# Mixing stage: the phases are made by GpSimd, and the products stand ahead of the powers

## The chip, the cores and the metric

The kernel runs on one core of one Trainium2 chip. The core has five engines with queues of their own: PE (TensorE, matrix products into the memory PSUM), DVE (VectorE), ACT (ScalarE), POOL (GpSimd) and SP, which here only issues transfers. They wait for one another by semaphores. The metric is the device time of one execution in microseconds (us), the median of three runs.

## The reference

A tower of one layer works on `x` of 32 x 128 x 64 complex numbers. A diagonal state space kernel makes 1024 positions out of 64 complex coefficients per row; then come attention with rotary positions and a layer with weights and activations rounded to 8 bits, each with a residual.

```python
dtA = A * dt[:, None]                      # A = -exp(inv_A_real) + 1j * A_imag, dt = exp(log_dt)
Cc = Bc[None, :, :] * Cc                   # Cc = x as complex numbers: (32, 128, 64)
Cc = Cc * (jnp.exp(dtA) - 1.0) / A
V = jnp.exp(dtA[:, :, None] * ell)         # ell = 0 .. 1023: (128, 64, 1024)
h = 2.0 * jnp.einsum('chn,hnl->chl', Cc, V).real
h = concatenate([cls_tok, h], axis=1)      # (32, 129, 1024)
h = h + attention(layernorm(h))            # 32 heads of 32, 8 for keys and values, causal
h = h + ffn(layernorm(h))                  # 1024 x 1024, both factors rounded to 8 bits, and a bias
```

## The kernel before

`program` runs three stages one behind the other: `mix_stage`, `attention_stage`, `ffn_stage`. The change touches `mix_stage` alone, which computes the einsum above.

A position l is split into a block j of 8 and an offset of 128 (PB) within it. For a row h the power exp(dtA * l) is the product of a block factor, which goes into the coefficients (tables `gr`, `gi`, turned by PE into `g_ps`), and a power of the offset, which goes into `eb`. The 128 rows h are worked in 8 chunks (NCP) of 16 (CP), each chunk k in two halves of 8 (CH). For one chunk:

- phases: for each of the 16 rows, one instruction iota * rate + quarter, 128x128, into `yb` (in pool_b). `turns_of`, DVE, L427.
- rounding: `kb`, the nearest whole number of the phases, 128x2048 (in pool_a). DVE, L432.
- subtraction: `yb` - `kb`, the fraction of a turn. POOL, L284. It waits for `wholes` and, by a second wait, for powers of the chunk before.
- sine: `sn` = sin(2 pi * fraction), 128x2048. ACT, L376, with a change of its function table before and after. For rows of even number the quarter turn makes it a cosine.
- magnitudes: 16 exponentials of 128x128 into `eb`. ACT, L368.
- powers: `eb` = `eb` * `sn`, 128x2048, both from SBUF. DVE, L422.
- products ("coefficients" in the code): `m1`, `m2` = input times coefficient, for one half of the chunk, two instructions of 128x2048, one factor from `g_ps` in PSUM. DVE, L523. They wait until PE has used up the same half of the chunk before (`rows_ready`).
- matrix products: per half four units of 8 matmuls of 128x128 into four PSUM banks. PE, L342; the profile records each as two. A unit waits until ACT has emptied its bank (`rows_out`).
- copies: ACT empties each bank into `ho` (L400), and SP stores it to `h_rows` in HBM, four stores a half.

`eb` has three buffers, `yb` two, `kb` and `sn` one, `m1` and `m2` one for each half. The order on each engine is written out by hand, and each engine works through its queue strictly in that order. DVE's order in a chunk is: phases and rounding of chunk k + 2, powers of chunk k + 1, both halves of products of chunk k + 1. ACT puts the magnitudes of chunk k + 2 behind the copies of the first half of chunk k, four rows a copy, and the sine of k + 2 behind them.

Before the loop there is a set-up of many small DVE instructions (exponentials, the coefficient tables through the helper `times`, copies into `dup`) beside the transposes of the input; its end is the turning of `dup` into `g_ps`, 16 transposes (L324), which wait for the whole of `dup` (`turn_in`).

Of the kernel before, what the change touches and what calls it, by code (L numbers as in the profile page):

```python
# [27 lines left out]
ALU = mybir.AluOpType  # L28
# [8 lines left out]
JB = 8  # L37
# [75 lines left out]
def at_least(eng, sem, value):  # L113

    if isinstance(value, int) and value <= 0:
        return
    eng.wait_ge(sem, value)
# [46 lines left out]
def mix_stage(nc, x, log_dt, B, inv_A, A_im, consts, h_dram, pool_a, pool_b, cst, ident_b, half_c, rows_stored,  # L164
# [6 lines left out]
    with ExitStack() as ctx:  # L171
# [3 lines left out]
        def sem(name):  # L175
            return ctx.enter_context(nc.semaphore("mix_" + name))
# [55 lines left out]
        turn_in = sem("turn_in")  # L232
        turned = sem("turned")
        turned_out = sem("turned_out")
        turns = sem("turns")
        wholes = sem("wholes")
        fracs = sem("fracs")
        mags = sem("mags")
# [37 lines left out]
        @block.gpsimd  # L276
        def _(pool):
            nc.gpsimd.memset(warm[:], 0.0).then_inc(warm_set, 1)
            nc.gpsimd.memset(warm_r[:].bitcast(F32), 0.0).then_inc(warm_set, 1)
            nc.gpsimd.memset(half_c[:], -0.5)  # L280
            for k in range(1, NCP):
                pool.wait_ge(wholes, k + 1)
                at_least(pool, powers_ready, k)
                nc.gpsimd.tensor_tensor(yb[:, k % 2], yb[:, k % 2], kb[:], ALU.subtract).then_inc(fracs, 1)  # L284

        @block.tensor
        def _(pe):
            pe.wait_ge(warm_set, 2)
            for j in range(4):
                nc.tensor.matmul(ps[0][32 * j:32 * j + 32, 0:2 * PB], warm[:, 0:32], warm[:], start=True, stop=True)  # L290
            for i in range(2):
                for j in range(4):
                    nc.tensor.matmul(ps[j][:, i * PB:(i + 1) * PB], warm_r[32 * j:32 * j + 32, 0:P],
                                     warm_r[32 * j:32 * j + 32, 0:PB], start=True, stop=True)

            pe.wait_ge(cst_loaded, 16)
            for r, (kind, i) in enumerate(TURNS):
                if kind == "x":
                    pe.wait_ge(x_loaded[i], 16)
                if kind == "small":  # L300
                    pe.wait_ge(turn_in, 1)
                if kind == "swap":
                    pe.wait_ge(turned_out, XR + 1)
                if r >= OUT_BANKS:
                    pe.wait_ge(turned_out, r - OUT_BANKS + 1)
                bank = ps[r % OUT_BANKS]
                if kind == "swap":
                    hs = NH // XR
                    mm = nc.tensor.matmul(bank[:], swap, c1[:, i * hs:(i + 1) * hs, :].rearrange("p h c -> p (h c)"),
                                          start=True, stop=True)  # L310
                elif kind == "x":
                    for q in range(4):
                        mm = nc.tensor.transpose(bank[:, q * P:(q + 1) * P],
                                                 xin[:, 4 * i + q].rearrange("h n r -> h (n r)"), ident)
                else:
                    for q, slot in enumerate((S_DECAY, S_TURN)):
                        mm = nc.tensor.transpose(bank[:, q * P:(q + 1) * P],
                                                 dup[:, slot].rearrange("h n r -> h (n r)"), ident)
                mm.then_inc(turned, 1)
            pe.wait_ge(turn_in, 2)  # L320
            for i in range(G_TURNS):
                for q in range(4):
                    part, slot = divmod(4 * i + q, JB)
                    mm = nc.tensor.transpose(g_ps[:, part, slot, :],  # L324
                                             dup[:, 4 * i + q].rearrange("h n r -> h (n r)"), ident)
                mm.then_inc(turned, 1)
            pe.wait_ge(turned_out, len(TURNS))

            for k in range(NCP):
                pe.wait_ge(powers_ready, k + 1)  # L330
                for half in range(2):
                    pe.wait_ge(products, 2 * k + half + 1)
                    for i in range(PAIRS):
                        at_least(pe, rows_out, unit(k, half, i) - OUT_BANKS + 1)
                        bank = ps[i]
                        for e in range(2):
                            for jj in range(2):
                                h = 2 * i + e
                                slots = slice(jj * (JB // 2), (jj + 1) * (JB // 2))
                                cols = slice((2 * e + jj) * PB, (2 * e + jj + 1) * PB)  # L340
                                for term in (m1, m2):
                                    mm = nc.tensor.matmul(bank[:, cols],  # L342
                                                          term[:, half, h, slots].rearrange("p j c -> p (j c)"),
                                                          eb[:, k % 3, half * CH + h, :],
                                                          start=term is m1, stop=term is m2)
                        mm.then_inc(rows_ready, 1)

        @block.scalar
        def _(act):
# [23 lines left out]
            def sine(k):  # L373
                act.wait_ge(fracs, k + 1)
                at_least(act, powers_ready, k)
                nc.scalar.activation(sn[:], yb[:, k % 2], ACT.Sin, scale=TWO_PI_DOWN).then_inc(sin_done, 1)  # L376
# [13 lines left out]
                magnitudes(0, 2 * i, 2)  # L390
            sine(0)
            magnitudes(1, 0, CP)
            sine(1)
            for k in range(NCP):
                for half in range(2):
                    if k >= 1:
                        act.wait_ge(rows_stored[half], 16 * JB // 2 * k)
                    for i in range(PAIRS):
                        act.wait_ge(rows_ready, unit(k, half, i + 1))
                        nc.scalar.copy(ho[:, half, 2 * i:2 * i + 2, :],  # L400
                                       ps[i][:].rearrange("p (e q) -> p e q", e=2)).then_inc(rows_out, 1)
                        if half == 0 and k + 2 < NCP:
                            magnitudes(k + 2, 4 * i, 4)
                    if half == 0 and k + 2 < NCP:
                        sine(k + 2)

        @block.vector
        def _(v):
            count = [0]

            def link(ins):

                count[0] += 1
                ins.then_inc(small, 1)
                v.wait_ge(small, count[0])
# [5 lines left out]
                v.wait_ge(sin_done, k + 1)  # L421
                V.tensor_tensor(eb[:, k % 3], eb[:, k % 3], sn[:], ALU.mult).then_inc(powers_ready, 1)  # L422

            def turns_of(k):
                at_least(v, sin_done, k - 1)
                for h in range(CP):
                    t = V.tensor_scalar(yb[:, k % 2, h, :], iota, rates[:, 1, k * CP + h:k * CP + h + 1],  # L427
                                        quarter, ALU.mult, ALU.add)
                t.then_inc(turns, 1)
                v.wait_ge(turns, k + 1)  # L430
                at_least(v, fracs, k)
                V.tensor_scalar(kb[:], yb[:, k % 2], MAGIC, -MAGIC, ALU.add, ALU.add).then_inc(wholes, 1)  # L432
                if k == 0:
                    v.wait_ge(wholes, 1)
                    V.tensor_tensor(yb[:, 0], yb[:, 0], kb[:], ALU.subtract).then_inc(fracs, 1)

            v.wait_ge(in_loaded, 48)

# [52 lines left out]
            V.scalar_tensor_tensor(s1[:], s1[:], 2.0, den[:], ALU.mult, ALU.mult)  # L491
            link(V.scalar_tensor_tensor(s2[:], s2[:], -2.0, den[:], ALU.mult, ALU.mult))

            def times(re, im, t, ar, ai, br, bi):

                V.tensor_tensor(re, ar, br, ALU.mult)
                link(V.tensor_tensor(t, ai, bi, ALU.mult))
                link(V.tensor_tensor(re, re, t, ALU.subtract))
                V.tensor_tensor(im, ar, bi, ALU.mult)
                link(V.tensor_tensor(t, ai, br, ALU.mult))  # L500
                link(V.tensor_tensor(im, im, t, ALU.add))
# [4 lines left out]
            for q in range(2):  # L506
                last = V.tensor_tensor(wj[:, q], wj[:, q], mag[:], ALU.mult)
            link(last)
            many = [P, JB - 1, NS]
            times(gr[:, 1:JB], gi[:, 1:JB], tw[:], gr[:, 0:1, :].to_broadcast(many), gi[:, 0:1, :].to_broadcast(many),  # L510
                  wj[:, 0], wj[:, 1])

            V.tensor_copy(dup[:, 0:JB, :, 0], gr[:])
            V.tensor_scalar(dup[:, 0:JB, :, 1], gr[:], -1.0, None, ALU.mult)
            for q in range(2):
                last = V.tensor_scalar(dup[:, JB:2 * JB, :, q], gi[:], -1.0, None, ALU.mult)
            last.then_inc(turn_in, 1)
# [12 lines left out]
            v.wait_ge(turned, ROUNDS)  # L530
            v.wait_ge(turned_out, len(TURNS))
            coefficients(0, 0)
            turns_of(1)
            coefficients(0, 1)
            for k in range(NCP):
                if k + 2 < NCP:
                    turns_of(k + 2)
                if k + 1 < NCP:
                    powers(k + 1)
                    coefficients(k + 1, 0)  # L540
                    coefficients(k + 1, 1)


def attention_stage(nc, cls, h_dram, ctx_dram, tail_dram, ml_dram, v0_dram, pool_a, x_end_r, weights_r, cst, half_c, h_stored,
# [1189 lines left out]
```

## Time and profile before

| | |
|---|---|
| median of 3 runs | 1680.6 us (1679.89 to 1681.06) |
| profiled execution | 1692.2 us |
| its span, first to last instruction | 1690.4 us |
| busy over the span: PE, DVE, ACT, POOL | 93%, 72%, 53%, 36% |
| chunk loop of the mixing stage, first to last matmul | 44.7 to 190.5 us |
| first matmul of the attention stage | 194.4 us |
| stores of the mixed rows | 64 of 256 KB, median 3.7 us from issue to landing |

The profiled execution is a run of its own and longer than the median by 11.6 us. PE's share hides what happens in the mixing stage, since that is a ninth of the span; there, the times of single instructions have to be read. A busy time is the sum of the drawn lengths, and matmuls are pipelined, so the step between them is shorter than their length. PEclk is the granted clock of TensorE as a share of 2.4 GHz: 0.50 is 1.2 GHz.

### The profile page before, as it was taken

Reading aid. Unit: us, or ns where it says so; the run is one execution under the profiler, and the core shown is the slowest. Engines: PE = TensorE matmul, PEld = TensorE weight load, DVE = VectorE, ACT = ScalarE, POOL = GpSimd, SP = SyncE. Lnnn points to the kernel's source line nnn. Section 1 sums busy time; section 2 is a strip of 40 time slices with the busy share of each in tenths; the row PEclk is TensorE's granted clock in tenths of the full one; section 3 lists DMA queues with packets and bytes.
Section 4 is the critical chain, followed back from the end, with each engine's and each line's share of the span. In section 5 each row is a group of like instructions: output and inputs, shape, how many; then the busy total and the mean of one; then the engine's idle time right before and its main releaser. Section 6 shows DMA issues by size and latency. Waiting matters only on the chain. (4 is left out here: it accounts for less than half of the span.)

```text
span 1690.4 us, 35578 instructions
## 1 busy us (share of the span) xinstructions
PE 1576.1 (93%) x11802; PEld 1254.9 (74%) x11802; DVE 1213.1 (72%) x2262; ACT 888.1 (53%) x2928; POOL 615.0 (36%) x632
## 2 busy tenths in 40 slices
PE   4888889999999999999999999937799999999997
PEld 2788868888888888888888888826577777777774
DVE  8997556676767666676767666537588888888885
ACT  7576427777777777777777777722311111111110
POOL 0322024444444444444444444410133333333333
PEclk8889989999999999999999999958899999999998
DMA  8345501101010101101010100043233233332221
GB/s 211 75 104 121 150 26 39 44 33 50 25 50 31 43 31 43 47 28 50 25 50 31 43 31 20 27 184 125 90 112 101 96 101 112 112 111 100 94 92 44
DMA packets 59160, 122.64 MB, mean 73 GB/s; under 512 B 9345, under 2 KB 29954, under 8 KB 59106
## 3 DMA queue, kind: packets, MB, share of 16 engines
q1 hardware_dynamic: 59106, 121.94, 23.1%
q8 instruction: 32, 0.52, 0.1%
q14 instruction: 22, 0.18, 0.0%
HBM read 71.18 MB, written 51.66 MB: 73 GB/s over the span
## 5 line engine op out<-in xcount | busy, mean ns | idle before, releaser
L764 POOL TENSOR_TENSOR pool_a<-pool_a,ri 128x512 f32<-128x512 f32 x256 | 266.4, 1041 | 459.4 <-DVE ri L1126 459.4
L984 ACT ACTIVATE pool_a<-sm,ml 128x128 f32<-128x128 f32 x1024 | 399.4, 396 | 19.7 <-DVE ml L1119 18.7
L836 PE MATMUL att_ps<-w_lo,xT_hi 128*128 128x512 f32 x768 | 325.9, 424 | 0.0
L836 PE MATMUL att_ps<-w_hi,xT_lo 128*128 128x512 f32 x768 | 304.2, 396 | 0.0
L836 PE MATMUL att_ps<-w_hi,xT_hi 128*128 128x512 f32 x768 | 304.1, 396 | 0.0
L1110 DVE TENSOR_TENSOR sm<-att_ps,cst 128x512 f32<-128x512 f32 x256 | 173.3, 677 | 142.6 <-PE att_ps L884 142.6
L997 ACT COPY pool_a<-att_ps 128x512 f32<-128x512 f32 x256 | 149.5, 584 | 164.0 <-PE att_ps L893 164.0
L1435 PE MATMUL ffn_ps<-wo_hi,cT_hi 128*128 128x512 f32 x528 | 215.6, 408 | 3.0 <-DVE cT_lo L1578 3.0
L1435 PE MATMUL ffn_ps<-wo_hi,cT_lo 128*128 128x512 f32 x528 | 206.8, 392 | 0.0
L1435 PE MATMUL ffn_ps<-wo_lo,cT_hi 128*128 128x512 f32 x528 | 206.0, 390 | 0.0
L984 ACT ACTIVATION_READ_ACCUMULATOR pool_a<-sm,ml 128x1 f32 x1024 | 196.6, 192 | 0.0
L1119 DVE TENSOR_REDUCE ml<-sm 128x4 f32<-128x512 f32 x256 | 176.3, 689 | 9.1
L1535 ACT COPY pool_b<-ffn_psb 128x1024 bf16<-128x1024 bf16 x33 | 33.4, 1012 | 276.2 <-PE ffn_psb L1452 276.1
L836 PEld LDWEIGHTS att_ps<-w_lo,xT_hi 128*128 128x128 f32 x768 | 145.2, 189 | 35.5 <-issue 11.9
L836 PEld LDWEIGHTS att_ps<-w_hi,xT_hi 128*128 128x128 f32 x768 | 145.1, 189 | 33.9
L836 PEld LDWEIGHTS att_ps<-w_hi,xT_lo 128*128 128x128 f32 x768 | 145.8, 190 | 23.1
L893 PE MATMUL att_ps<-cst,pool_a 128*128 128x128 f32 x1024 | 157.9, 277 | 2.6 <-ACT pool_a L997 2.6
L893 PEld LDWEIGHTS att_ps<-cst,pool_a 128*128 128x128 f32 x1024 | 122.8, 141 | 36.9 <-issue 2.0
L342 PE MATMUL mix_ps<-eb,pool_b 128*128 128x128 f32 x1024 | 127.3, 291 | 23.1 <-ACT pool_b L400 18.5
L1418 POOL TENSOR_TENSOR pool_b<-pool_b 128x1024 f32<-128x1024 f32 x33 | 79.4, 2406 | 180.6 <-DVE pool_b L1604 164.7
L342 PEld LDWEIGHTS mix_ps<-eb,pool_b 128*128 128x128 f32 x1024 | 125.8, 207 | 24.8 <-issue 23.9
L1461 PE MATMUL ffn_ps<-wq,pool_b 128*128 128x512 bf16 x528 | 124.1, 390 | 2.2 <-ACT pool_b L1535 2.2
(213 smaller groups left out, 2510.5 us busy)
## 6 DMA issues: line engine op xcount, KB each, us to landing
h_in<-h_rows SPq DMA_DIRECT2D x33, 512.0 KB, 4.3
h_rows<-pool_b SPq DMA_DIRECT2D x64, 256.0 KB, 3.7
hbuf<-h_rows SPq DMA_DIRECT2D x32, 512.0 KB, 3.7
ctx_turned<-pool_a SPq DMA_DIRECT2D x64, 256.0 KB, 2.0
ctx_in<-ctx_turned SPq DMA_DIRECT2D x32, 512.0 KB, 3.6
out_dram<-pool_b SPq DMA_DIRECT2D x32, 512.0 KB, 2.8
pool_a<-in_L_attn_Wq_dram SPq DMA_DIRECT2D x8, 512.0 KB, 18.2
pool_b<-in_L_attn_Wo_dram SPq DMA_DIRECT2D x2, 2048.0 KB, 13.4
```

The lines of the kernel that those rows point to most:

```text
L342: mm = nc.tensor.matmul(bank[:, cols], term[:, half, h, slots].rearrange("p j c -> p (j c)"), eb[:, k % 3, half * CH + h, :], start=term i ...
L764: G.tensor_tensor(pr[:, g % 4], pr[:, g % 4], ri[:, g % 2, :].unsqueeze(2).to_broadcast([P, GQ, P]), ALU.mult).then_inc(p_ready, 1)
L836: mm = nc.tensor.matmul(bank[:], lhs, w_part[:, e, blk * BK:(blk + 1) * BK], start=(r == 0), stop=(r == EC * 3 - 1))
L893: mm = nc.tensor.transpose(PT_BANK[:, q * P:(q + 1) * P], pr[:, g % 4, q, :], ident)
L984: a = nc.scalar.activation(pr[:, g % 4, q, :], sm[:, g % 2, q, :], ACT.Exp, bias=ml[:, b[1], 0, h:h + 1], accum_out=ml[:, b[1], 1, h:h + 1])
L997: nc.scalar.copy(pT[:, g // 4, g % 4, :], PT_BANK[:]).then_inc(p_stored, 1)
L1110: V.tensor_tensor(sm[:, g % 2], S_BANK[g % 4][:].rearrange("p (q k) -> p q k", q=GQ), cst[:, C_MASK:C_MASK + P].unsqueeze(1).to_broadcast( ...
L1119: V.tensor_reduce(ml[:, b[1], 0, heads_of(g)], sm[:, g % 2], AX.X, ALU.max, negate=True).then_inc(negmax_ready, 1)
L1418: nc.gpsimd.tensor_tensor(yo[:, c[1], :], ya[:, c[1], :], hb[:, c[1], :], ALU.add).then_inc(out_ready, 1)
L1435: mm = nc.tensor.matmul(O_BANK[half][:], c_part[:, t[1], e, :], w_part[:, e, half * BK:(half + 1) * BK], start=(e == 0 and part == 0), sto ...
L1461: mm = nc.tensor.matmul(Y_BANK[half][:], xqT[:, c[1], e, :], wq8[:, e, half * BK:(half + 1) * BK], start=(e == 0), stop=(e == EC - 1))
L1535: nc.scalar.copy(xqT[:, c[1], :, :].rearrange("p c k -> p (c k)"), psb[:]).then_inc(xq_stored, 1)
```

## The change

Four edits, all in `mix_stage`. First, the phases of chunks 1 to 7 are made by POOL (L284 of the new file) instead of DVE; chunk 0's stay on DVE. POOL's queue becomes: wait for the first powers, phases of 1, and then for each chunk its subtraction and the phases of the next. The subtraction no longer waits for powers. Second, DVE's order in a chunk becomes: products of the first half, powers, rounding of the next chunk, products of the second half. Third, ACT spreads the magnitudes over both halves (four rows behind each of the first two copies of a half) and puts the sine of the next chunk behind the third copy of the first half; the second sine no longer comes before the loop. Fourth, in the set-up the real tables are written to `dup` as soon as the real part is there, and PE turns them while DVE makes the imaginary part.

```diff
@@ gpsimd
+            def phase(k):
+                at_least(pool, sin_done, k - 1)
+                for h in range(CP):
+                    t = nc.gpsimd.tensor_scalar(yb[:, k % 2, h, :], iota, rates[:, 1, k * CP + h:k * CP + h + 1],
+                                                quarter, ALU.mult, ALU.add)
+                t.then_inc(phases, 1)
+
+            def fraction(k):
+                pool.wait_ge(wholes, k + 1)
+                nc.gpsimd.tensor_tensor(yb[:, k % 2], yb[:, k % 2], kb[:], ALU.subtract).then_inc(fracs, 1)
+
+            pool.wait_ge(powers_ready, 1)
+            phase(1)
             for k in range(1, NCP):
-                pool.wait_ge(wholes, k + 1)
-                at_least(pool, powers_ready, k)
-                nc.gpsimd.tensor_tensor(yb[:, k % 2], yb[:, k % 2], kb[:], ALU.subtract).then_inc(fracs, 1)
+                fraction(k)
+                if k + 1 < NCP:
+                    phase(k + 1)
@@ tensor
-            pe.wait_ge(turn_in, 2)
             for i in range(G_TURNS):
+                if i % (G_TURNS // 2) == 0:
+                    pe.wait_ge(turn_in, 2 + 2 * i // G_TURNS)
@@ scalar
             magnitudes(1, 0, CP)
-            sine(1)
             for k in range(NCP):
                 for half in range(2):
...
-                        if half == 0 and k + 2 < NCP:
-                            magnitudes(k + 2, 4 * i, 4)
-                    if half == 0 and k + 2 < NCP:
-                        sine(k + 2)
+                        if i < 2 and k + 2 < NCP:
+                            magnitudes(k + 2, 8 * half + 4 * i, 4)
+                        if half == 0 and i == 2 and k + 1 < NCP:
+                            sine(k + 1)
@@ vector
-            def turns_of(k):
-                at_least(v, sin_done, k - 1)
-                for h in range(CP):
-                    t = V.tensor_scalar(yb[:, k % 2, h, :], iota, rates[:, 1, k * CP + h:k * CP + h + 1],
-                                        quarter, ALU.mult, ALU.add)
-                t.then_inc(turns, 1)
-                v.wait_ge(turns, k + 1)
+            def whole(k):
+                v.wait_ge(phases, k + 1)
                 at_least(v, fracs, k)
                 V.tensor_scalar(kb[:], yb[:, k % 2], MAGIC, -MAGIC, ALU.add, ALU.add).then_inc(wholes, 1)
...
+            def real_tables():
+                V.tensor_copy(dup[:, 0:JB, :, 0], gr[:])
+                V.tensor_scalar(dup[:, 0:JB, :, 1], gr[:], -1.0, None, ALU.mult).then_inc(turn_in, 1)
+
             times(gr[:, 1:JB], gi[:, 1:JB], tw[:], gr[:, 0:1, :].to_broadcast(many), gi[:, 0:1, :].to_broadcast(many),
-                  wj[:, 0], wj[:, 1])
-
-            V.tensor_copy(dup[:, 0:JB, :, 0], gr[:])
-            V.tensor_scalar(dup[:, 0:JB, :, 1], gr[:], -1.0, None, ALU.mult)
+                  wj[:, 0], wj[:, 1], real_tables)
+
...
             coefficients(0, 0)
-            turns_of(1)
+            whole(1)
             coefficients(0, 1)
-            for k in range(NCP):
-                if k + 2 < NCP:
-                    turns_of(k + 2)
+            for k in range(1, NCP):
+                coefficients(k, 0)
+                powers(k)
                 if k + 1 < NCP:
-                    powers(k + 1)
-                    coefficients(k + 1, 0)
-                    coefficients(k + 1, 1)
+                    whole(k + 1)
+                coefficients(k, 1)
```

How the rows of DVE move, from the first powers on. In the kernel before (L422 powers, L523 products, L427 phases, L432 rounding; `eb` the powers, pool_a the sine or the rounded phases, mix_g the coefficients in PSUM):

```order
L422 TENSOR_TENSOR eb<-eb,pool_a 128x2048
L523 TENSOR_TENSOR pool_b<-pool_b,mix_g 128x2048 x2
L427 TENSOR_SCALAR pool_b<-cst,rates 128x128 x16
L432 TENSOR_SCALAR pool_a<-pool_b 128x2048
L523 TENSOR_TENSOR pool_b<-pool_b,mix_g 128x2048 x2
L427 TENSOR_SCALAR pool_b<-cst,rates 128x128 x16
L432 TENSOR_SCALAR pool_a<-pool_b 128x2048
L422 TENSOR_TENSOR eb<-eb,pool_a 128x2048
L523 TENSOR_TENSOR pool_b<-pool_b,mix_g 128x2048 x4
```

And in the changed kernel (L435 powers, L541 products, L440 rounding):

```order
L435 TENSOR_TENSOR eb<-eb,pool_a 128x2048
L541 TENSOR_TENSOR pool_b<-pool_b,mix_g 128x2048 x2
L440 TENSOR_SCALAR pool_a<-pool_b 128x2048
L541 TENSOR_TENSOR pool_b<-pool_b,mix_g 128x2048 x4
L435 TENSOR_TENSOR eb<-eb,pool_a 128x2048
L440 TENSOR_SCALAR pool_a<-pool_b 128x2048
```

The phases are gone from DVE; of each four products two stand ahead of powers, and the rounding stands between powers and the other two.

On ACT, from the sine before the loop on. In the kernel before (L376 sine with its table, L368 magnitudes with theirs, L400 copies):

```order
L376 ACT_TABLE_LOAD
L376 ACTIVATE pool_a<-pool_b 128x2048
L400 COPY pool_b<-mix_ps 128x512
L368 ACT_TABLE_LOAD
L368 ACTIVATE eb<-cst,rates 128x128 x4
L400 COPY pool_b<-mix_ps 128x512
L368 ACTIVATE eb<-cst,rates 128x128 x4
L400 COPY pool_b<-mix_ps 128x512
L368 ACTIVATE eb<-cst,rates 128x128 x4
L400 COPY pool_b<-mix_ps 128x512
L368 ACTIVATE eb<-cst,rates 128x128 x4
L376 ACT_TABLE_LOAD
```

And in the changed kernel (L390 sine, L382 magnitudes, L413 copies), from the first copy on:

```order
L413 COPY pool_b<-mix_ps 128x512
L382 ACTIVATE eb<-cst,rates 128x128 x4
L413 COPY pool_b<-mix_ps 128x512
L382 ACTIVATE eb<-cst,rates 128x128 x4
L413 COPY pool_b<-mix_ps 128x512
L390 ACT_TABLE_LOAD
L390 ACTIVATE pool_a<-pool_b 128x2048
L413 COPY pool_b<-mix_ps 128x512 x2
L382 ACT_TABLE_LOAD
L382 ACTIVATE eb<-cst,rates 128x128 x4
L413 COPY pool_b<-mix_ps 128x512
L382 ACTIVATE eb<-cst,rates 128x128 x4
```

The sine stands behind the third copy now, and the other eight magnitudes behind the first copies of the second half.

## Rows read from the trace of the kernel before

**Rows 1.** Busy time by stage: the end of the set-up, the chunk loop.

```profile
36.20:44.70 8.50, 3.68 (x16) 3.28 (x17) 6.93 (x5) 3.63 (x9) 0.00 (x0) 0.50 0.05 12
44.70:190.50 145.80, 127.28 (x1024) 125.84 (x1024) 119.14 (x156) 89.91 (x179) 31.81 (x7) 0.91 0.46 109
```

**Rows 2.** Timeline of PE: start us, length us, line, what, xcount, [idle before].

```profile
36.38 3.68 PE L324 MATMUL mix_g<-cst,pool_b 128*128 128x128 f32 x16 [10.78 <-DVE pool_b L516]
44.73 9.10 PE L342 MATMUL mix_ps<-eb,pool_b 128*128 128x128 f32 x64 [4.67 <-DVE pool_b L523]
140.25 14.53 PE L342 MATMUL mix_ps<-eb,pool_b 128*128 128x128 f32 x128 [0.44 <-ACT pool_b L400]
159.14 31.32 PE L342 MATMUL mix_ps<-eb,pool_b 128*128 128x128 f32 x256 [4.36 <-ACT pool_b L400]
```

**Rows 3.** Waits, 36 to 192 us: who <- for whom, us, times, longest.

```profile
PE mix_ps L342 <- ACT pool_b L400: 18.5, 7, 5.0
ACT pool_a L376 <- POOL pool_b L284: 27.1, 7, 14.7
```

**Rows 4.** Timeline of DVE through one chunk, from 104 us.

```profile
104.58 4.49 DVE L523 TENSOR_TENSOR pool_b<-pool_b,mix_g 128x2048 f32<-128x2048 f32 x2 [2.66 <-PE mix_ps L342]
108.98 4.19 DVE L427 TENSOR_SCALAR pool_b<-cst,rates 128x128 f32<-128x128 f32 x16
113.20 1.23 DVE L432 TENSOR_SCALAR pool_a<-pool_b 128x2048 f32<-128x2048 f32 x1
114.34 2.28 DVE L422 TENSOR_TENSOR eb<-eb,pool_a 128x2048 f32<-128x2048 f32 x1
116.54 8.87 DVE L523 TENSOR_TENSOR pool_b<-pool_b,mix_g 128x2048 f32<-128x2048 f32 x4
```

**Rows 5.** Timeline of POOL and ACT in the same chunk.

```profile
116.77 4.53 POOL L284 TENSOR_TENSOR pool_b<-pool_b,pool_a 128x2048 f32<-128x2048 f32 x1 [15.40 <-DVE eb L422]
121.33 1.91 ACT L376 ACTIVATE pool_a<-pool_b 128x2048 f32<-128x2048 f32 x1 [3.35 <-POOL pool_b L284]
128.00 1.28 ACT L368 ACT_TABLE_LOAD   x1
```

**Rows 6.** Timeline of DVE, end of the set-up.

```profile
36.24 2.28 DVE L422 TENSOR_TENSOR eb<-eb,pool_a 128x2048 f32<-128x2048 f32 x1
40.09 4.49 DVE L523 TENSOR_TENSOR pool_b<-pool_b,mix_g 128x2048 f32<-128x2048 f32 x2 [1.57 <-PE mix_g L324]
```

**Rows 7.** Groups of small and large POOL instructions, and one of DVE.

```profile
L777 POOL COPY pool_a<-pool_a 128x4 f32 x52 | 9.9, 191 | 0.0
L278 POOL MEMSET warm<- 128x256 f32 x1 | 0.3, 311 | 0.3 <-POOLq L1723 0.3
L759 POOL TENSOR_TENSOR pool_a<-pool_a 128x256 f32<-128x256 f32 x32 | 23.7, 740 | 5.0 <-DVE pool_a L1092 5.0
L759 POOL TENSOR_TENSOR pool_a<-pool_a 128x512 f32<-128x512 f32 x64 | 81.7, 1276 | 6.3 <-DVE pool_a L1092 6.3
L435 DVE TENSOR_TENSOR pool_b<-pool_b,pool_a 128x2048 f32<-128x2048 f32 x1 | 2.3, 2293 | 0.0
```

**Rows 8.** Timeline of POOL: two instructions of one kind, one behind the other.

```profile
216.88 0.95 POOL L807 MEMSET x_end_hi<- 128x1024 f32 x1 [3.58 <-ACT w_hi L1037]
217.77 0.95 POOL L807 MEMSET x_end_lo<- 128x1024 f32 x1
```

**Rows 9.** DVE lines over the span: duration ns min/median/max, first and last start.

```profile
L1578 DVE TENSOR_TENSOR cT_lo<-ctx_in,cT_hi x64: 675/684/1879, 1159.4 to 1634.4; 128x512 fp32r<-128x512 f32 x64
L1585 DVE TENSOR_SCALAR pool_b<-pool_b,ffn_mv,ffn_rstd x33: 806/2873/2879, 1176.2 to 1669.7; 128x1024 f32<-128x1024 f32 x33
L523 DVE TENSOR_TENSOR pool_b<-pool_b,mix_g x32: 2280/2281/2289, 40.1 to 178.4; 128x2048 f32<-128x2048 f32 x32
```

**Rows 10.** Timeline of POOL and of DVE around 1265 us.

```profile
1265.53 2.39 POOL L1412 TENSOR_TENSOR pool_b<-pool_b,pool_a 128x1024 f32<-128x1024 f32 x1
1265.60 2.87 DVE L1585 TENSOR_SCALAR pool_b<-pool_b,ffn_mv,ffn_rstd 128x1024 f32<-128x1024 f32 x1 [0.67 <-POOL ffn_rstd L1408]
```

More of the change, by code:

```diff
@@ L234, in mix_stage @@
         turned_out = sem("turned_out")
-        turns = sem("turns")
+        phases = sem("phases")
         wholes = sem("wholes")
@@ L422, in powers, with turns_of @@
                 V.tensor_tensor(eb[:, k % 3], eb[:, k % 3], sn[:], ALU.mult).then_inc(powers_ready, 1)
-            def turns_of(k):
-                at_least(v, sin_done, k - 1)
-                for h in range(CP):
-                    t = V.tensor_scalar(yb[:, k % 2, h, :], iota, rates[:, 1, k * CP + h:k * CP + h + 1],
-                                        quarter, ALU.mult, ALU.add)
-                t.then_inc(turns, 1)
-                v.wait_ge(turns, k + 1)
+            def whole(k):
+                v.wait_ge(phases, k + 1)
                 at_least(v, fracs, k)
                 V.tensor_scalar(kb[:], yb[:, k % 2], MAGIC, -MAGIC, ALU.add, ALU.add).then_inc(wholes, 1)
-                if k == 0:
-                    v.wait_ge(wholes, 1)
-                    V.tensor_tensor(yb[:, 0], yb[:, 0], kb[:], ALU.subtract).then_inc(fracs, 1)
+            def turns_of(k):
+                for h in range(CP):
+                    t = V.tensor_scalar(yb[:, k, h, :], iota, rates[:, 1, k * CP + h:k * CP + h + 1],
+                                        quarter, ALU.mult, ALU.add)
+                t.then_inc(phases, 1)
+                whole(k)
+                v.wait_ge(wholes, k + 1)
+                V.tensor_tensor(yb[:, k], yb[:, k], kb[:], ALU.subtract).then_inc(fracs, 1)
             v.wait_ge(in_loaded, 48)
@@ L492, in _, with times @@
             link(V.scalar_tensor_tensor(s2[:], s2[:], -2.0, den[:], ALU.mult, ALU.mult))
-            def times(re, im, t, ar, ai, br, bi):
+            def times(re, im, t, ar, ai, br, bi, between=lambda: None):
                 V.tensor_tensor(re, ar, br, ALU.mult)
@@ L498, in times @@
                 link(V.tensor_tensor(re, re, t, ALU.subtract))
+                between()
                 V.tensor_tensor(im, ar, bi, ALU.mult)
```

## The prediction

> **What bounds the kernel now.** I read the busy time by stage first, then the timeline of PE, then who waited for whom, then DVE, POOL and ACT through one chunk. The change touches only the mixing stage. Its chunk loop runs from 44.7 to 190.5 us and holds 127.3 us of PE, 119.1 of DVE, 89.9 of ACT and 31.8 of POOL, at a granted clock of 0.91 [rows 1]: no engine is full. The timeline of PE says what full would be: an undisturbed chunk is 128 recorded matmuls in 14.5 us, while the first half chunk, after 4.7 us of idle, needs 9.1 us for 64, and the last two chunks, after a gap of 4.4 us, need 31.3 where undisturbed ones need 29 [rows 2]. So the loop's 145.8 us are about 8 x 14.4 = 115 us of work (14.5 less the drawn-out end of the last matmul), 18.5 us of gaps and some 12 us of matmuls at a lower clock. All seven gaps end with a copy of ACT, 18.5 us [rows 3]. ACT is late because it stands in front of its sine: 27.1 us it waited there for POOL's subtraction [rows 3]. One chunk shows the chain. DVE ends powers at 116.6, POOL's subtraction starts only then and takes 4.53 us, the sine starts at 121.3 [rows 4, 5]. DVE itself is what powers waits behind: per chunk 4.2 us of phases, 1.2 of rounding, 2.3 of powers and 8.9 of products [rows 4], 16.6 us before any wait, more than PE's 14.4. Two things hold the loop, then: DVE's load, and the chain powers, subtraction, sine, copies.
>
> **The change, part by part.**
>
> The set-up. The first eight transposes of the coefficients can start after the real tables, while DVE still makes the imaginary ones. Today all 16 run from 36.4 for 3.7 us at clock 0.50 [rows 1, 2] and DVE waits for them until 40.1, though its powers end at 38.5 [rows 6]. Eight will be over before 36.4, the other eight end near 38.2, so the first products start at 38.5 instead of 40.1: 1.6 us gained, and PE's first half chunk starts near 43.05 instead of 44.7. It comes after about as long an idle as now, so it keeps its 9.1 us.
>
> DVE. Seven times the 4.2 us of phases leave it (chunk 0's stay). 12.4 us per chunk remain, 2 us under PE's 14.4. The products of the first half now stand ahead of powers. The cycle that must close within a chunk is: PE does one half (7.2), which frees the product buffers; DVE makes the next products (4.5) and then powers (2.2 more); with 0.15 us of handing over (44.58 to 44.73, DVE's end to PE's start) this is 14.05. It closes with 0.35 us to spare. The rounding comes behind powers, and behind it the other half's products, which PE wants only half a chunk later: 1.2 + 4.4 us against 7.2.
>
> ACT. Its work per chunk is unchanged, 89.9 / 8 = 11.2 us [rows 1], but the exponentials are spread over both halves, and the sine comes behind the third copy of the first half. Each chunk still changes tables twice (1.28 us each [rows 5], in the 11.2). At that copy, 5.4 us into a chunk, the subtraction must be done: it is a rounding and 4.55 us behind powers, thus 5.8. The sine then ends about 9 us in, powers needs it at 12. The fourth copy is delayed to about 9.5, PE wants that bank back at 12.6. No wait of PE there.
>
> POOL. It takes over 7 x 16 phase instructions of 128x128, a form that no row shows here. I call its step from start to start t. From below: a copy of 4 elements takes 191 ns, and a memset grows from 311 ns for 256 elements to 0.95 us for 1024, 0.83 ns each; 191 + 124 x 0.83 = 0.29 us, of which 0.06 overlap with the next, since two memsets of 0.95 start 0.89 apart [rows 7, 8]. That is 0.23, with nothing for the two scalars read from memory. From above: two-tensor additions take 740 ns at 256 and 1276 at 512 elements, 2.09 each, so 0.47 at 128 [rows 7]. Another upper end: the 128x2048 subtraction takes 4.53 us on POOL and 2.29 on DVE [rows 5, 7], a ratio of 1.98, and DVE's phases step by 4.22 / 16 = 0.264 [rows 4]; that makes 0.52. Scalars from memory could put t above all of these. I take 0.38, midway between 0.29 and 0.47. 16t is then 6.1 us per chunk.
>
> What POOL's serial chain allows: in each chunk rounding (1.23), subtraction (4.55), phases of the chunk after next (16t), and powers (2.28), because the next rounding stands behind powers on DVE. The period is 8.06 + 16t, 14.15 us at t = 0.38: just under PE's 14.4. Written out from the end of the first powers: 38.5 + 7 x (1.23 + 4.55 + 16t) + 6 x 2.28 + 3.2 (last table and sine) + 2.3 (last powers) + 14.4 (last chunk on PE) = 112.6 + 112t. PE alone gives 43.05 + 9.1 + 7.2 + 7 x 14.4 = 160.2. The two meet at t = 0.425, and the chain reaches today's 190.5 at t = 0.70.
>
> Does POOL's reading hinder DVE? The rows say yes for two kinds of DVE instruction. One with a single tensor but a fast rate, 128x1024, takes 0.81 us undisturbed and 2.87 when POOL's 2.39 us addition started 0.07 us before it; one with two tensors from SBUF goes from 0.68 up to 1.88 [rows 9, 10]. The products read one tensor from PSUM, and all 32 keep 2.28 us although POOL's subtraction runs beside some [rows 9]. Powers reads two tensors from SBUF and now comes near POOL's phases. At t = 0.38 these end 5.8 + 6.1 = 11.9 us after the powers before, and powers wants to start at 12.0. If they meet, it waits for one phase instruction, 0.4 us at most, which the spare 0.35 nearly covers. I charge 0.15 us x 7 = 1 us.
> The Trainium skill, page "SBUF — State Buffer", section "Who interferes with whom", says this as a rule: a VectorE instruction with two SBUF inputs and a GpSimd one that reads SBUF shut each other out for a whole instruction. The trace agrees; by that rule the cost is the same 1 us, since each phase instruction is short.
>
> Transfers. The stores of the mixed rows kept the DMA engines at 0.46 of the loop [rows 1]; packed into 118 us that is 0.57, not a bound. The attention stage starts when the last rows are stored, at a fixed distance from the last copy, so what the loop gains arrives at the end of the program.
>
> Sum: the last matmul of the stage at 160.2 + 1 = 161.2 instead of 190.5, 29.3 us less. The profiled execution took 1692.2 us (span 1690.4), so 1662.9; it lies 11.6 us above the median of the runs, and I carry the difference over in microseconds: 1680.6 - 29.3 = 1651.
>
> **Rivals.**
>
> A, the forecast: PE becomes the bound, or POOL passes it by a hair, t up to 0.46. 1649 to 1655.
>
> B: POOL becomes the bound. For it: a kind of instruction it has not run here, and the ratio of 1.98 to DVE. At t = 0.523 the stage ends at 112.6 + 58.6 = 171.2, and the gain is 19.3: 1661. DVE then waits at the rounding with products behind it, and PE for the products. Against it: the ratio is that of two-tensor work, and POOL's small instructions are cheap. It holds from t = 0.46 to 0.67, 1655 to 1677.
> The Trainium skill, "GPSIMD Engine Reference", section "Engine selection", advises VectorE for elementwise work, calling GpSimd about twice as slow for two inputs but near line rate for one. By the factor of two for this kernel, B is what comes; by the one-input half of the sentence, A. Its section on elementwise cycle accounting has 769 ns for 512 elements in a good loop, from which I estimate 0.19 us for 128 and no delay at all. No run here shows either for this form.
>
> C, slower: the same instructions cost much more, because each fetches two scalars per partition. Place: POOL between subtraction and rounding. The price is 112 us for each microsecond of t, and it decides from t = 0.70. At t = 0.82 the stage ends at 204.4: 1694. If powers and phases did not exclude one another the chain would be 13.7 us shorter and the turning point 0.82. Against it: it needs nearly three times DVE's step.
>
> D: the gaps of PE stay in part, though POOL is quick enough. The sine still stands between two copies; if the subtraction comes a microsecond or two late there, or the clock drops again at each small gap, PE loses 1.5 us per chunk: 161.2 + 10.5 = 171.7, gain 18.8, 1662. For it: every gap today ends at a copy [rows 3], and the spare times above (0.35, 0.25 us) are thin. Against it: copies have 3 us of room through the four banks.
>
> **Chances.** A 0.57, B 0.26, C 0.08, D 0.09. The forecast is A's, 1651. What a measurement can tell here from no change is 0.2%, 3.4 us. C and half of B's far tail lie at or above that: faster 0.89, same 0.03, slower 0.08. For 8 in 10 the range takes in A with its lower bound (t = 0.23 gains nothing more, but powers undelayed and a first half at full clock would give 1646) and B and D up to t = 0.62: 1646 to 1671.
>
> **What would show it.** POOL's group of phase instructions: its mean and step give t at once. PE in the loop: 1024 matmuls without a gap above 1 us after the first chunk, granted clock near 1, the last ending near 161. ACT's wait for POOL before the sine falls from 27.1 us to a few. DVE's wait for POOL at the rounding: small in A, several us per chunk in B and C. Powers of 2.28 us stay so, or grow by up to 0.4 where phases run beside them. The set-up: first products at 38.5. I am wrong if t is above 0.46, or if PE waits more than 0.5 us per chunk for DVE or ACT while t is below that.

## The result, and the profile after

The changed kernel takes 1657.2 us (1656.5 to 1658.1, 4 runs) against 1680.4: a ratio of 0.9862, 95% interval 0.9845 to 0.9879, 23.2 us less. The forecast was 1651, 29.3 us less, in a range of 1646 to 1671.

PE in the mixing stage, the view of [rows 2] (timeline: start, length, what, xcount, idle before):

```profile
33.86 1.97 PE L338 MATMUL mix_g<-cst,pool_b 128*128 128x128 f32 x8 [8.32 <-DVE pool_b L528]
36.38 1.67 PE L338 MATMUL mix_g<-cst,pool_b 128*128 128x128 f32 x8 [0.56 <-DVE pool_b L534]
43.06 67.28 PE L356 MATMUL mix_ps<-eb,pool_b 128*128 128x128 f32 x576 [5.01 <-DVE pool_b L541]
110.67 14.56 PE L356 MATMUL mix_ps<-eb,pool_b 128*128 128x128 f32 x128 [0.32 <-DVE pool_b L541]
125.49 14.56 PE L356 MATMUL mix_ps<-eb,pool_b 128*128 128x128 f32 x128 [0.26 <-DVE pool_b L541]
140.31 21.71 PE L356 MATMUL mix_ps<-eb,pool_b 128*128 128x128 f32 x192 [0.26 <-DVE pool_b L541]
```

The stage's last matmul ends at 162.0 us (forecast 161.2, before 190.5). The seven gaps before ACT's copies are gone. PE runs its first 576 matmuls, four chunks and a half, without a gap; after that it waits 0.3 us for products once in each chunk.

POOL and DVE through one chunk, the views of [rows 4, 5]; the first row is POOL's very first set of phases:

```profile
38.63 6.88 POOL L284 TENSOR_SCALAR pool_b<-cst,rates 128x128 f32<-128x128 f32 x16 [37.30 <-DVE eb L435]
...
106.31 4.56 POOL L290 TENSOR_TENSOR pool_b<-pool_b,pool_a 128x2048 f32<-128x2048 f32 x1 [1.35 <-DVE pool_a L440]
110.84 8.94 POOL L284 TENSOR_SCALAR pool_b<-cst,rates 128x128 f32<-128x128 f32 x16
121.12 4.56 POOL L290 TENSOR_TENSOR pool_b<-pool_b,pool_a 128x2048 f32<-128x2048 f32 x1 [1.34 <-DVE pool_a L440]
```

```profile
106.14 8.87 DVE L541 TENSOR_TENSOR pool_b<-pool_b,mix_g 128x2048 f32<-128x2048 f32 x4
114.93 2.39 DVE L435 TENSOR_TENSOR eb<-eb,pool_a 128x2048 f32<-128x2048 f32 x1
119.81 1.23 DVE L440 TENSOR_SCALAR pool_a<-pool_b 128x2048 f32<-128x2048 f32 x1 [2.50 <-POOL pool_b L284]
120.96 8.87 DVE L541 TENSOR_TENSOR pool_b<-pool_b,mix_g 128x2048 f32<-128x2048 f32 x4
```

Alone, 16 phases take 6.88 us, a step of t = 0.43 us from start to start. With powers among them they take 8.94: POOL stands still while DVE reads two tensors from SBUF. DVE has finished powers at 117.3 and then waits 2.5 us for POOL before the rounding. POOL itself never rests but for the rounding: 4.53 + 8.94 + 1.34 = 14.8 us, and that is the period of the loop here (106.31 to 121.12). It is a little above the 14.33 us that PE needs for a chunk (measured in warm5, below).

The two kinds of instruction over the span (duration ns min/median/max), and after them the waits that are left between 30 and 175 us (us in total, times, longest), the view of [rows 3]:

```profile
L284 POOL TENSOR_SCALAR pool_b<-cst,rates x112: 442/453/2571, 38.6 to 134.2; 128x128 f32<-128x128 f32 x112
L435 DVE TENSOR_TENSOR eb<-eb,pool_a x8: 2281/2385/2548, 36.2 to 144.6; 128x2048 f32<-128x2048 f32 x8
```

```profile
DVE pool_a L440 <- POOL pool_b L284: 13.8, 7, 2.6
ACT pool_b L413 <- DMA h_rows<-pool_b: 10.0, 7, 2.0
...
PE mix_ps L356 <- DVE pool_b L541: 5.9, 4, 5.0
...
ACT pool_a L390 <- POOL pool_b L290: 0.3, 1, 0.3
```

ACT waited 27.1 us for the subtraction before its sine [rows 3]; now it waits 0.3 us.

### The profile page after: what moved, and what is told of

Its sections match the earlier page's. It is cut to its first block and busy times, and to the rows that moved or that the text cites. A ratio compares the mean times of both kernels' runs of the same rounds, so it can differ in the third digit from the quotient of the medians.

```text
span 1656.3 us, 35571 instructions
## 1 busy us (share of the span) xinstructions
PE 1560.1 (94%) x11802; PEld 1242.6 (75%) x11802; DVE 1184.2 (71%) x2150; ACT 888.0 (54%) x2928; POOL 675.5 (41%) x744
## 5 line engine op out<-in xcount | busy, mean ns | idle before, releaser
L356 PE MATMUL mix_ps<-eb,pool_b 128*128 128x128 f32 x1024 | 118.1, 279 | 5.9 <-DVE pool_b L541 5.9
L356 PEld LDWEIGHTS mix_ps<-eb,pool_b 128*128 128x128 f32 x1024 | 117.1, 195 | 6.9 <-issue 5.2
```

What stands on the lines that cost most here:

```text
L356: mm = nc.tensor.matmul(bank[:, cols], term[:, half, h, slots].rearrange("p j c -> p (j c)"), eb[:, k % 3, half * CH + h, :], start=term i ...
```

## Experiments

**r_before and r_after: both kernels once more.** No edit. The first two profiled executions, one of each kernel, differed by 34.1 us, the medians by 23.2.

> The kernel before, once more, with a profile. The first profiled execution of it was 11.6 us longer than the median of its runs, while the changed kernel's is within 1 us of its own median; the two traces differ by 34.1 us, the medians by 23.2. Theory 1 (the lengths of the clock's low stretches vary between executions of the kernel before, whose seven gaps of the mixing stage sit at the edge of dropping it): a second profile ends the mixing stage some us earlier than 190.5, at 183 to 188, with a granted clock above 0.91 in the loop, and its own time is near 1680. Theory 2 (the mixing stage is the same in each execution, and the extra is elsewhere, in attention or the last stage, or the profile's own cost): the stage ends at 190.5 again, within 0.5 us.

> The changed kernel once more. Both theories: 1657 +- 1, the mixing stage's last matmul ends at 162.0 +- 1, since it has no gaps in which the clock could drop; POOL's phase step 0.43 us, period of a chunk 14.85.

Measured: 1682.0 and 1657.6 us. PE in the second profile of the kernel before (an execution of 1681.5 us):

```profile
57.16 9.25 PE L342 MATMUL mix_ps<-eb,pool_b 128*128 128x128 f32 x64 [3.54 <-ACT pool_b L400]
69.26 14.53 PE L342 MATMUL mix_ps<-eb,pool_b 128*128 128x128 f32 x128 [2.85 <-ACT pool_b L400]
...
139.95 16.16 PE L342 MATMUL mix_ps<-eb,pool_b 128*128 128x128 f32 x128 [5.04 <-ACT pool_b L400]
156.32 28.82 PE L342 MATMUL mix_ps<-eb,pool_b 128*128 128x128 f32 x256 [0.22 <-ACT pool_b L400]
```

Here the stage ends at 185.1, not 190.5, with 16.5 us of gaps instead of 18.5 and matmuls of 124 us instead of 127.3. Theory 1 holds as far as one more profile can show it: the stage of the kernel before varies from execution to execution. Its 12 runs lie between 1680.6 and 1692.1 us, the longest with a mean granted clock of 0.960, the others 0.965 to 0.969. The changed kernel ends its stage at 162.0 in both profiles, and 185.1 - 162.0 = 23.1 us agrees with the measured gain of 23.2.

The stage explains only half of what lies between the two profiles of the kernel before (spans of 1690.4 and 1679.8 us). The other 5.3 us come later, most of them where the attention hands over to the last layer. The 110 us from 900 us after the attention's first matmul, first profile and second (window, its length, busy us and number of PE, PEld, DVE, ACT and POOL, granted clock, DMA share, GB/s):

```profile
1094.40:1204.40 110.00, 63.15 (x402) 49.52 (x401) 62.26 (x96) 38.77 (x86) 13.73 (x14) 0.73 0.38 138
1089.10:1199.10 110.00, 61.73 (x418) 49.37 (x418) 64.32 (x98) 37.71 (x81) 15.18 (x14) 0.80 0.39 140
```

A long execution is not special to a kernel with gaps in this stage: split4 and phases_half below, whose profiled loops have no gap, each have one of 1663.5 and 1661.9 us, 6 to 8 us above their medians. Where those two lose it was not profiled.

**setup_alone: the early real tables in the kernel before.**

```diff
+                if i % (G_TURNS // 2) == 0:
+                    pe.wait_ge(turn_in, 2 + 2 * i // G_TURNS)
...
+                between()     # real_tables(), ahead of the imaginary part
```

> The kernel before with only the set-up edit (real tables written and turned early). Theory: DVE's first products start at 38.45 instead of 40.1 and everything behind moves by 1.6 us: about 1678.8, ratio 0.999. Rival: the first half chunk on PE starts earlier but waits for the same later things (DVE's phases of chunk 1 stay between the products), and the gain is lost in the first gap: ratio 1.000, the first gap 1.6 us longer. As the clock's low stretches may shift, +-3 us either way.

Measured: ratio 0.9994 (0.9985 to 1.0003). The first matmul of the loop starts at 42.95 instead of 44.74, the last ends at 187.6, within the spread of the kernel before. The 1.8 us are there still at the start of chunk 1 (67.47 instead of 69.26 in r_before), so they are not lost in the first gap, as the rival had it. Whether they reach the end, this run can't tell.

**order_only: the new orders with the phases on DVE.**

```diff
-            phase(1)                                        # on POOL, with all further phases
...
+                if k > 0:                                   # in whole(k), on DVE
+                    at_least(v, sin_done, k - 1)
+                    for h in range(CP):
+                        t = V.tensor_scalar(yb[:, k % 2, h, :], iota, rates[:, 1, k * CP + h:k * CP + h + 1],
+                                            quarter, ALU.mult, ALU.add)
+                    t.then_inc(phases, 1)
```

> The changed kernel with all phases back on DVE, directly ahead of each rounding; the new orders of DVE and ACT and the set-up stay. Theory (DVE's load bounds it): 16 x 0.264 = 4.2 us more per chunk on DVE, 16.6 to 17 us per chunk against 14.85, so the stage ends 7 x 1.9 = 13 us later, at 175: 1670. Rival (the order did all the work, phases on DVE would have fitted into its waits): the stage ends within 3 us of 162: 1657 to 1660. Second rival (the products of the second half come so late that PE idles long enough to lose its clock): 182 or later, 1677.

Measured: 1671.7 us (1666.9 to 1675.5), ratio 0.9938 (0.9919 to 0.9957); the stage ends at 173.2. DVE in one chunk:

```profile
90.33 2.29 DVE L424 TENSOR_TENSOR eb<-eb,pool_a 128x2048 f32<-128x2048 f32 x1
92.53 4.19 DVE L430 TENSOR_SCALAR pool_b<-cst,rates 128x128 f32<-128x128 f32 x16
96.76 1.23 DVE L435 TENSOR_SCALAR pool_a<-pool_b 128x2048 f32<-128x2048 f32 x1
97.90 8.87 DVE L536 TENSOR_TENSOR pool_b<-pool_b,mix_g 128x2048 f32<-128x2048 f32 x4
```

DVE runs without a pause, 16.36 us a chunk: its load bounds the loop, as the theory says. Against 185.1 the stage is 12 us shorter, from the orders and the set-up without the offload. By the times the gain is 10.4 us (ratio 0.9938); the profiled execution was the longest of the six, 1675.5 us, with the same low clock of 0.73 at the hand-over to the last layer as the first profile of the kernel before.

**pool_only: the phases on POOL, all orders as before.**

```diff
+            phase(1)
...
-                at_least(pool, powers_ready, k)
                 nc.gpsimd.tensor_tensor(yb[:, k % 2], yb[:, k % 2], kb[:], ALU.subtract).then_inc(fracs, 1)
+                if k + 1 < NCP:
+                    phase(k + 1)
...
-                at_least(v, sin_done, k - 1)                # in turns_of(k), on DVE
+                if k == 0:                                  # its 16 phase instructions for chunk 0 alone
```

> The kernel before with only the phases of chunks 1 to 7 moved to POOL (and the subtraction no longer waiting for powers); the orders of DVE and ACT and the set-up stay as before. Theory 1 (the offload alone lifts both limits: DVE's load falls to 12.4 us per chunk, and POOL's chain of rounding, subtraction, phases and powers is the same 14.85 us): the stage's last matmul at 162 + 1.6 for the set-up, up to 167 with a few stumbles; 1659 to 1663. Theory 2 (the products must stand ahead of powers and the sine between the copies, or the gaps before ACT's copies stay): gaps of 2 to 4 us at ACT's copies in most chunks, the stage ends at 175 or later; 1670 or more.

Measured: 1670.1 us, ratio 0.9931 (0.9916 to 0.9946); the stage ends at 173.6. PE:

```profile
68.68 31.33 PE L352 MATMUL mix_ps<-eb,pool_b 128*128 128x128 f32 x256 [6.12 <-ACT pool_b L410]
...
115.30 14.53 PE L352 MATMUL mix_ps<-eb,pool_b 128*128 128x128 f32 x128 [0.22 <-ACT pool_b L410]
130.05 14.53 PE L352 MATMUL mix_ps<-eb,pool_b 128*128 128x128 f32 x128 [0.22 <-ACT pool_b L410]
```

and POOL's subtraction, and ACT's second sine, ahead of its first copy:

```profile
59.62 6.50 POOL L292 TENSOR_TENSOR pool_b<-pool_b,pool_a 128x2048 f32<-128x2048 f32 x1 [1.35 <-DVE pool_a L442]
```

```profile
51.45 1.91 ACT L386 ACTIVATE pool_a<-pool_b 128x2048 f32<-128x2048 f32 x1 [11.19 <-POOL pool_b L292]
```

Neither theory holds as it stands. In the steady state theory 1 does: 14.75 us a chunk with gaps of 0.2. But the start costs what theory 2 asked for: the second sine keeps ACT from its first copy until 53.3, everything behind is late, and PE then waits 6.1 us ahead of chunk 1 and runs at a lower clock behind it (31.3 us for 256 matmuls instead of 28.8). Chunk 1 starts at 68.7, in the changed kernel at 59.8: 8.9 of the 11.6 us between the two stages' ends are lost by then, 1.6 of them to the old set-up. So once the phases are on POOL, the new orders are worth little in the steady state and much at the start. Which of them brings it (the second sine out of the way is the obvious one) no run here tells apart. In this kernel powers meets the subtraction instead of the phases: the subtraction takes 6.50 us instead of 4.55, so the two exclude each other there too.

**powers_first: DVE's order turned back in the changed kernel.**

```diff
-                coefficients(k, 0)
                 powers(k)
                 if k + 1 < NCP:
                     whole(k + 1)
+                coefficients(k, 0)
                 coefficients(k, 1)
```

> The changed kernel with DVE's order turned back: powers and rounding ahead of both products in a chunk; phases on POOL, ACT's new order and the set-up as changed. Theory (the products must stand ahead of powers, since powers now waits for a sine that comes 9 us into the chunk, and behind it the products of the first half are late): PE waits 2 to 3 us for products in each chunk, period 17, the stage ends at 175 to 178: 1671 to 1674. Rival (the order of DVE is without effect once the phases are gone): 162 and 1658.

Measured: 1690.7 us, ratio to before 1.0053 (1.0039 to 1.0067): slower than the kernel before, and 17 us beyond my theory's upper end. The stage ends at 194.9. PE, and the longest wait of DVE:

```profile
66.24 16.27 PE L356 MATMUL mix_ps<-eb,pool_b 128*128 128x128 f32 x128 [7.29 <-issue]
85.44 14.53 PE L356 MATMUL mix_ps<-eb,pool_b 128*128 128x128 f32 x128 [2.94 <-issue]
102.91 16.16 PE L356 MATMUL mix_ps<-eb,pool_b 128*128 128x128 f32 x128 [2.94 <-issue]
122.00 17.34 PE L356 MATMUL mix_ps<-eb,pool_b 128*128 128x128 f32 x128 [2.94 <-issue]
142.29 17.44 PE L356 MATMUL mix_ps<-eb,pool_b 128*128 128x128 f32 x128 [2.94 <-issue]
```

```profile
DVE eb L435 <- ACT pool_a L390: 44.7, 7, 8.2
```

The mechanism is the theory's: DVE stands up to 8.2 us before powers, waiting for the sine, with both products behind it. PE's gaps end as those products do (102.8 us for the gap that ends at 102.91), though the profile names no releaser. The price was too small. The gap of 2.94 us is as long as expected, but a low clock follows it in most chunks (15.9 to 17.4 us for 128 matmuls instead of 14.5), and slower matmuls make the next sine later; the first of the gaps, 7.29 us, was not in the theory at all. DVE's order and ACT's are a pair: the new place of the sine with the old order of DVE loses more than the offload gives.

**phases_more and phases_half: the load of POOL up and down.** The first adds 8 phase instructions per chunk on POOL, into memory that nobody reads. The second makes only 8 of the 16; it leaves out the phases of half of the rows, and nothing takes their place.

```diff
+                for h in range(8):          # phases_more
...                                          # spare: a part of gr or gi
+                    nc.gpsimd.tensor_scalar(spare, iota, rates[:, 1, k * CP + h:k * CP + h + 1], quarter,
+                                            ALU.mult, ALU.add)
...
-                for h in range(CP):
+                for h in range(0, CP, 2):   # phases_half
```

> The changed kernel with 8 more phase instructions per chunk on POOL, into memory that nobody reads, ahead of the 16. Theory (serial chain on POOL, period 8.06 + n x 0.43 with n the number of phase instructions): 3.44 us more in each of 7 chunks, period 18.3, the stage ends at 162 + 24 = 186: 1681. Rival (the chain is not serial with powers and had slack): less than 2.3 us per chunk, the stage ends before 178. Second rival (PE's clock drops in the new gaps of 3.8 us and adds 1.5 us per chunk): no effect on the end while POOL sets the pace, since PE's half chunk is done long before the next products.

> The changed kernel with only 8 of the 16 phase instructions per chunk on POOL; the other rows' phases are left out, nothing takes their place. Theory (PE is next behind POOL): POOL's period falls to 11.5 us, PE's matmuls run without a gap, 128 in 14.33, and the stage ends at 43.0 + 9 + 7.2 + 7 x 14.33 = 159.5 to 160.2, 2 us earlier: 1655 to 1656. Rival (another wait of 0.3 us per chunk stands right behind, such as the cycle of products and powers with its 14.05 us): 161 to 162, no change.

Measured: 1682.9 us, ratio 1.0013 (1.0001 to 1.0024), stage to 186.1; and 1655.5 us, ratio 0.9855 (0.9837 to 0.9873), stage to 160.1. POOL with 24, then PE with 8:

```profile
105.22 4.53 POOL L294 TENSOR_TENSOR pool_b<-pool_b,pool_a 128x2048 f32<-128x2048 f32 x1 [1.35 <-DVE pool_a L444]
109.73 3.48 POOL L285 TENSOR_SCALAR pool_a<-cst,rates 128x128 f32<-128x128 f32 x8
113.16 8.97 POOL L288 TENSOR_SCALAR pool_b<-cst,rates 128x128 f32<-128x128 f32 x16
123.47 4.54 POOL L294 TENSOR_TENSOR pool_b<-pool_b,pool_a 128x2048 f32<-128x2048 f32 x1 [1.34 <-DVE pool_a L444]
```

```profile
43.06 117.08 PE L356 MATMUL mix_ps<-eb,pool_b 128*128 128x128 f32 x1024 [4.79 <-DVE pool_b L541]
```

The period with 24 is 18.25 us (expected 18.3), the end 186.1 (expected 186): the chain is serial and each 0.43 us counts in full. Three of its chunks take PE 16.1 to 17.1 us for 128 matmuls behind gaps of 3.7 us, and the end does not move by it, as the second rival says. With 8, PE never stops, and the stage ends 1.9 us before the changed kernel's: that is what POOL's load costs there.

**split4: four phase rows of each chunk back on DVE.**

```diff
-                for h in range(CP):
+                for h in range(4, CP):                      # POOL
...
+                    for h in range(4):                      # DVE, in whole(k)
+                        t = V.tensor_scalar(yb[:, k % 2, h, :], iota, rates[:, 1, k * CP + h:k * CP + h + 1],
+                                            quarter, ALU.mult, ALU.add)
+                    t.then_inc(own, 1)
+                    v.wait_ge(own, k)
```

> The changed kernel with 4 of each chunk's 16 phase rows given back to DVE, made just ahead of the rounding. Theory (POOL's chain of 14.85 us is the bound by a hair over PE's 14.5): POOL's share falls by 4 x 0.43 = 1.7 us, DVE's rises by 1.1 to 13.5, PE becomes the bound; its gaps of 0.3 us vanish, the stage ends 1.5 to 2.5 us earlier, at 160: 1655 to 1656.5, ratio to the changed kernel 0.999. Rival (DVE's phase instructions and POOL's shut one another out, and the rounding comes no earlier): the stage ends at 162 to 163.

Measured: 1656.0 us (1653.9 to 1663.5, 5 runs), ratio 0.9855 (0.9836 to 0.9874). The interval overlaps that of the changed kernel, so the times do not show it to be faster; the trace shows the stage 1.7 us shorter, with the whole loop in one piece:

```profile
43.08 117.22 PE L357 MATMUL mix_ps<-eb,pool_b 128*128 128x128 f32 x1024 [4.72 <-DVE pool_b L549]
```

POOL is relieved by more than the 1.7 us of four instructions: a set of 12 is over as powers starts (its longest instruction takes 0.53 us, none waits through powers), so the 2.1 us of standing still are gone too.

**warm5: split4, and PE kept busy ahead of the loop.**

```diff
             pe.wait_ge(turned_out, len(TURNS))
+            for _ in range(5):
+                nc.tensor.matmul(ps[0][:, 0:2 * PB], warm[:, 0:P], warm[:], start=True, stop=True)
```

> split4 (4 of 16 phase rows of each chunk on DVE) with five more matmuls of 128x256 on PE between the last transposes of the set-up and the first products, on a tile of zeros, into a bank that nobody reads before it is written again. They fill the 4.9 us in which PE idles from 38.1 to 43.06. Theory (the first half chunk, 64 recorded matmuls in 9 to 10 us instead of 7.2, is slow only because PE idles ahead of it): it takes 7.2 to 7.5 us, the stage ends 2 us earlier, at 158.2: 1653.5 to 1654.5. Rival (the new matmuls run at the low clock, take more than 4.9 us and delay the first products, or the clock does not rise): the first unit starts later than 43.1 and the stage ends at 160.3 or later.

Measured: 1652.4 us (1650.7 to 1653.4), ratio 0.9825 (0.9811 to 0.9838), the fastest version here, and its interval lies below that of the changed kernel; it still overlaps that of split4, from which it differs only by the new matmuls, so against split4 the trace decides.

```profile
38.06 2.70 PE L344 MATMUL mix_ps<-warm 128*128 128x256 f32 x10
42.98 114.62 PE L359 MATMUL mix_ps<-eb,pool_b 128*128 128x128 f32 x1024 [2.23 <-DVE pool_b L551]
```

All 1024 matmuls now run at the rate of 14.33 us per 128, and the stage ends at 157.6. The new ones fill 2.7 us and leave a gap of 2.2, and the clock does not fall in it. The stretch of the first half chunk in the changed kernel and in warm5 (the fields as above):

```profile
43.00:52.60 9.60, 9.54 (x65) 9.57 (x66) 5.62 (x3) 5.12 (x12) 8.26 (x10) 0.75 0.01 2
43.00:50.30 7.30, 7.30 (x65) 7.30 (x66) 6.60 (x7) 5.19 (x12) 5.85 (x4) 1.00 0.00 0
```

The clock is granted at 1.00 where the changed kernel has 0.75.

## Why the prediction was right, and where not

The bound. PE sets the pace for four and a half chunks, and POOL's chain for the rest, at 14.8 us a chunk against PE's 14.33. Rival A named this, "POOL passes it by a hair"; it is the seam to B. The forecast of the stage's end, 161.2, missed by 0.8, and this is in part luck. PE alone ends at 160.1 (phases_half) where the sum had 160.2. What comes on top is 1.9 us from POOL's chain, which the sum put at nothing; in its place the sum had 1 us for a wait of powers that did not matter.

The step t. Taken as 0.38, it measured 0.43, within the bounds 0.23 to 0.52 and just above the 0.425 at which POOL's chain passes PE. The chain's period, 8.06 + 16t, gives 14.94 and was 14.8; phases_more confirms its slope with 3.4 us for eight more instructions. So rival B's mechanism came true, at a price of 1.9 us (phases_half) instead of 10. Rivals C and D did not come; what C needed, t = 0.70, is far off, and PE no longer waits for a copy, as D had it.

POOL beside DVE. I charged 1 us for powers waiting on a phase instruction. Powers grew by 0.1 in the median and 0.27 at most, and DVE then waits for POOL anyway. The large side of the exclusion is POOL's: in six of the seven sets, all but the first, one phase instruction waits through powers (up to 2.57 us instead of 0.45). The sum had this size, since the chain counted powers as serial, but the reason that it gave, "because the next rounding stands behind powers on DVE", is not what the trace shows: DVE is through with powers 2.5 us before the rounding may start. It is the exclusion that makes powers a part of POOL's chain. In split4 and phases_half no phase instruction waits through powers, and there the formula would not hold. The Trainium skill, page "SBUF — State Buffer", section "Who interferes with whom", has the loser blocked for a whole instruction. The trace agrees: 6.88 us of phases become 8.94 beside a powers of 2.39.

Set-up. First products at 38.44, as forecast (38.5); PE's loop from 43.06 (43.05). That PE keeps its slow start was right (about 9.6 us for the first half chunk, forecast 9.1), and warm5 shows what that costs: 2.7 us.

The orders. I priced them only by what they would allow. order_only and pool_only show that each half of the change brings about half the gain: 12 us of the stage each against the 185.1 of the second profile, 10.4 and 11.6 us by the ratios of the times.

The term that was mis-sized is the last: "I carry the difference over in microseconds". The sum was made against a profiled execution whose stage ends at 190.5 us. In the second profile, of an execution 1 us above the median, it ends at 185.1, and I take that for the usual one. The profiled run lay 11.6 us above the median, and I took that as an offset that both kernels share. It was not: 5.4 of it was in the very stage that the change shortens, in gaps and low clock that differ between the two profiles; most of the rest came after it (1496.0 us from the attention's first matmul to the end, against 1490.7 in the second profile). 162.0 in place of 161.2 accounts for 0.8 of the missing 6.1 us, this for 5.4.

## What to carry to other kernels

When a profiled execution is longer than the median, look for the extra inside the stage that the change touches, and take it off the gain. Here the stage with gaps ended 5.4 us apart in two profiles, the changed one, with gaps of 0.3 us, at 162.0 in both. Moving work to a slower engine pays in full as long as its whole serial chain, with the time in which it must not read, stays under the period of the bound; where it lies a little above, the last few instructions are better shared, which the trace of split4 shows and its times do not contradict. The place of a producer in one queue (ACT's sine) and of its consumer in another (powers) have to be moved together: with the sine moved and powers not, the kernel was slower than before any change. The reverse, powers moved and the sine not, was not run.

## What the runs showed of the hardware

A POOL instruction that multiplies 128x128 f32 by one scalar per partition and adds another takes 0.45 us and steps by 0.43; DVE's steps by 0.264 [rows 4]. So for one input of this size POOL is 1.63 times slower, not 1.98 as for the 128x2048 subtraction. Five matmuls on zeros ahead of the loop moved the stage's end from 160.3 to 157.6, so the first half chunk, 7.2 us at the full clock, had taken about 9.9. ACT waits 1.2 to 2.0 us a chunk for the stores of the chunk before, 10.0 us in all. The prediction did not see this wait, and it costs nothing: PE no longer waits for ACT in the loop.
